# The second layer's linear-attention branch, moved tile by tile into the edge pass that sums gathered rows

## The reference

```python
def _L1_gnn_ref(x, edge_index, W, b):
    src = concat([edge_index[0], loop]); dst = concat([edge_index[1], loop])
    norm = deg_inv_sqrt[src] * deg_inv_sqrt[dst]
    h = x @ W.T
    out = segment_sum(h[src] * norm[:, None], dst, N) + b
    return relu(out)

def _L1_mix_ref(x, Wq, Wk, Wv, Wm, W1, W2, g1, b1, g2, b2):   # 8 heads of 32
    Q, K = elu(x @ Wq) + 1, elu(x @ Wk) + 1;  v = x @ Wv
    KV = einsum('nshd,nshv->nhdv', K, v)
    Z = 1 / (einsum('nlhd,nhd->nlh', Q, K.sum(axis=1)) + 1e-6)
    msg = layernorm(heads_joined(Q, KV, Z) @ Wm, g1, b1)
    msg = layernorm(relu(concat([x, msg]) @ W1) @ W2, g2, b2)
    return x + msg

xn = layernorm(x)
x = x + _L1_gnn_ref(xn, ...) + _L1_mix_ref(xn[None], ...)[0]
```

## Time and profile before

| what | value |
|---|---|
| median of three runs | 14292.15 us (14256.97 to 14311.86) |
| profiled execution | 14272.68 us, its span 14270.9 us |
| PE busy | 7573.7 us, 53% of the span |
| DVE busy | 6386.1 us, 45% |
| POOL busy | 6037.2 us, 42% |
| ACT busy | 1225.8 us, 9% |
| mean granted clock of PE | 0.773 of full speed |

### The profile page before, as it was taken

How to read it: one execution, slowest core, us unless ns; L and a number is a source line. 1 busy time by engine, 2 the same in 40 slices (tenths; PEclk the granted TensorE clock), 3 DMA queues, 4 the chain that set the end, 5 groups by cost and what they waited for, 6 DMA issues and landing times. The chain is left out here.

```text
span 14270.9 us, 106989 instructions
## 1 busy us (share of the span) xinstructions
PE 7573.7 (53%) x30362; PEld 6003.4 (42%) x30362; DVE 6386.1 (45%) x16883; ACT 1225.8 (9%) x3131; POOL 6037.2 (42%) x6226
## 2 busy tenths in 40 slices
PE   3334432556665455685555564555571955666534
PEld 3333332345554355553343432433351844555423
DVE  6555654467885322320000434666632134444454
ACT  0000000000001100110000111000010210110001
POOL 1666465056662266306666003666501016666000
PEclk9999999767777555697777787777785977777767
DMA  1111111055664011103336001112503313336100
GB/s 40 55 50 56 36 55 40 19 166 170 173 176 84 10 8 8 11 23 93 92 92 85 10 6 31 45 45 46 39 9 81 111 62 95 94 94 89 26 8 15
DMA packets 455094, 872.31 MB, mean 61 GB/s; under 512 B 171930, under 2 KB 267396, under 8 KB 454154
## 3 DMA queue, kind: packets, MB, share of 16 engines
q0 software_dynamic: 277568, 621.62, 20.3%
q1 hardware_dynamic: 176960, 244.01, 5.6%
HBM read 821.23 MB, written 52.88 MB: 61 GB/s over the span
## 5 line engine op out<-in xcount | busy, mean ns | idle before, releaser
L552 POOL DMA_INDIRECT ee_rows<-e_table,net_mr_data x1000 | 993.5, 993 | 1271.9 <-POOLq L1405 691.3
L817 POOL DMA_INDIRECT ce_rows<-c_table,net_mr_data x1000 | 948.2, 948 | 979.8 <-SPq L810 505.8
L552 POOL DMA_INDIRECT ge_rows<-g_table,net_mr_data x1000 | 961.0, 961 | 670.8 <-issue 233.1
L387 POOL DMA_INDIRECT main_slots<-em_load,em_where x784 | 808.9, 1032 | 641.9 <-DVE em_where L362 388.5
L552 POOL DMA_INDIRECT ae_rows<-a_table,net_mr_data x752 | 726.2, 966 | 590.7 <-POOLq L1405 200.7
L552 POOL DMA_INDIRECT be_rows<-b_table,b_br_data x728 | 703.1, 966 | 428.7 <-issue 176.8
L589 PE MATMUL ee_part_ps<-ee_message,net_eye 125*125 125x256 f32 x2000 | 588.8, 459 | 451.2 <-issue 258.3
L589 PE MATMUL ge_part_ps<-ge_rows,net_eye 125*125 125x256 f32 x2000 | 626.8, 482 | 308.2 <-issue 163.3
L346 PE MATMUL em_look_ps<-em_table,em_hot_tT 25*128 25x125 f32 x1568 | 366.9, 421 | 732.1 <-issue 662.6
L828 PE MATMUL ce_part_ps<-ce_rows,net_eye 125*125 125x256 f32 x2000 | 599.2, 452 | 289.9 <-issue 195.7
L589 PEld LDWEIGHTS ee_part_ps<-ee_message,net_eye 125*125 125x125 f32 x2000 | 461.1, 235 | 560.2 <-issue 467.6
(11 more groups left out here) (1010 smaller groups left out, 16655.6 us busy)
## 6 DMA issues: line engine op xcount, KB each, us to landing
em_key_row<-main_keys SPq DMA_DIRECT2D x98, 512.0 KB
f_w<-in_L_ffn_W_dram SPq DMA_DIRECT2D x40, 1024.0 KB
eg_key_row<-gat_keys SPq DMA_DIRECT2D x64, 512.0 KB
ce_rows<-c_table,net_mr_data POOLq DMA_INDIRECT x1000
ee_rows<-e_table,net_mr_data POOLq DMA_INDIRECT x1000
ge_rows<-g_table,net_mr_data POOLq DMA_INDIRECT x1000
main_slots<-em_load,em_where POOLq DMA_INDIRECT x784
ae_rows<-a_table,net_mr_data POOLq DMA_INDIRECT x752
```

Of the source, the lines that this page charges most:

```text
L387: pool.indirect_dma_start(edge["slots"], bass.IndirectOffsetOnAxis(ap=where[:, c:c + 1], axis=0), load[:, c, :], None).then_inc(scattered, 16)
L552: pool.indirect_dma_start(rows[n][:, s, :], None, table, bass.IndirectOffsetOnAxis(ap=data[:, g, s, 0:1].bitcast(I32), axis=0)).then_inc(g ...
L817: pool.indirect_dma_start(rows[:, g % RING, s, :], None, table, bass.IndirectOffsetOnAxis(ap=data[:, g, s, 0:1].bitcast(I32), axis=0)).the ...
```

## The change

The attention branch is no longer a row of stages behind the pass. `sum_pass` gets the rest of its work beside the 8 gathers of each group. A helper, `beside`, decides in turn i of every engine's loop which pieces run:

- from turn 2 on, one tile a turn: k and v of tile t in one product of 512 columns, its elu, and its share of the gram matrix (25 tiles, turns 2 to 28);
- in turn 29 the gram matrix is masked by heads on DVE (a mask made beforehand on POOL);
- from turn 29 on, one tile every 3 turns, cut into stages s0 to s11, each of which is one turn later than the one before it: q (s0), elu (s1), turn (s2), heads (s3), turn (s4), Wm and its statistics (s5), root and normalising (s5, s6), turn with gain and shift (s7), hidden layer (s8), output and statistics (s9), normalising (s10), the addition to `X` (s11). The last piece runs in turn 29 + 72 + 11 = 112 of 125.

All nine weight transfers are issued by SP at the start of the pass; ACT and DVE wait for all of them before their first group. `X` receives `A` and the last shift `b2` before the pass, in the same block in which the table is stored; the separate fill block is gone, and `close` keeps three of its four operations. On PE the pieces come behind `sum_slots(i)` and `total(i - 1)` in the turn, later stages before earlier ones; a piece waits for what ACT or DVE did with the same tile in the turn before. On DVE the addition to `acc` now comes one turn later in the loop.

```diff
--- before.py
+++ after.py
@@ -795,18 +795,56 @@
...
-def sum_pass(nc, edge, table, width, acc, const, name):
+def sum_pass(nc, edge, table, acc, XT, X, heads, weights, const, name):
...
-        rows = k.sb("rows", [128, RING, SLOTS, width])
-        hot, part = k.sb("hot", [128, HOTS, 2 * NP]), k.sb("part", [128, PARTS, width])
...
+        def beside(i, **stages):
+
+            if "gram" in stages and 0 <= i - FIRST - 2 < T:
+                stages["gram"](i - FIRST - 2)
+            if "keys" in stages and 0 <= i - FIRST - 1 < T:
+                stages["keys"](i - FIRST - 1)
+            if "kv" in stages and 0 <= i - FIRST < T:
+                stages["kv"](i - FIRST)
+            if "keep_gram" in stages and i == FIRST + T + 2:
+                stages["keep_gram"]()
+            for s in range(STAGES - 1, -1, -1):
+                t, off = divmod(i - SECOND - s, EACH)
+                if off == 0 and 0 <= t < T and f"s{s}" in stages:
+                    stages[f"s{s}"](t)
+
...
+            @block.sync
+            def _(sp):
+                for q, (to, of) in enumerate(((wkv[:, :, 0:D], "Wk"), (wkv[:, :, D:512], "Wv"), (wq[:, :, :], "Wq"), (wm[:, :, :], "Wm"))):
+                    sp.dma_start(to, weights[of].rearrange("(q p) n -> p q n", p=128)).then_inc(loaded, 16)
+                sp.dma_start(w1[:, :, :], weights["W1"][0, :, :].rearrange("(q p) n -> p q n", p=128)).then_inc(loaded, 16)
+                sp.dma_start(w2[:, :, :], weights["W2"][0, :, :].rearrange("(q p) n -> p q n", p=128)).then_inc(loaded, 16)
+                for to, of in ((g1, "g1"), (b1, "b1")):
+                    sp.dma_start(to[:, :], weights[of]).then_inc(loaded, 16)
+                sp.dma_start(g2[0:NP, :], along(weights["g2"], NP)).then_inc(loaded, 16)
+
+            LOADS = 16 * 9
+
...
+                def kv(t):
+                    if t == 0:
+                        pe.wait_ge(loaded, LOADS)
+                    if t >= 2:
+                        pe.wait_ge(k_made, t - 1)
+                    for q in range(2):
+                        ins = pe.matmul(bank[t % 2][0:NP, :], XT[:, q, tile(t)], wkv[:, q, :], start=(q == 0), stop=(q == 1))
+                    ins.then_inc(kv_made, 1)
...
+                def gram(t):
+                    pe.wait_ge(k_made, t + 1)
+                    pe.wait_ge(kv_out, t + 1)
+                    for m in range(2):
+                        ins = pe.matmul(bank[2 + m][:, 0:D + 1], k_t[0:NP, t % 2, m * 128:(m + 1) * 128], v_t[0:NP, t % 2, :], start=(t == 0), stop=(t == T - 1))
+                    ins.then_inc(grammed, 1)
...
+                def queries(t):
+                    if t == 0:
+                        pe.wait_ge(k_made, T)
+                    else:
+                        pe.wait_ge(qT_kept, t)
+                    times(bank[0][0:NP, 0:D], [XT[:, q, tile(t)] for q in range(2)], wq, q_made)
...
+                    pe.wait_ge(qT_kept, t + 1)
+                    if t == 0:
+                        pe.wait_ge(gram_kept, 1)
+                    else:
+                        pe.wait_ge(mT_kept, t)
+                    times(bank[1][0:NP, 0:D + 8], [qT[:, q, 0:NP] for q in range(2)], grams, m_made)
...
+                def mixed(t):
+                    pe.wait_ge(mT_kept, t + 1)
+                    if t:
+                        pe.wait_ge(nT_kept, t)
+                    times(bank[2][0:NP, 0:D], [mT[:, q, 0:NP] for q in range(2)], wm, w_made)
...
+                def hidden(t):
+                    pe.wait_ge(nT_kept, t + 1)
+                    if t:
+                        pe.wait_ge(y_kept, t)
+                    of = [XT[:, q, tile(t)] for q in range(2)] + [nT[:, q, 0:NP] for q in range(2)]
+                    for m in range(4):
+                        for q in range(4):
+                            ins = pe.matmul(bank[3][:, m * NP:(m + 1) * NP], w1[:, q, m * 128:(m + 1) * 128], of[q], start=(q == 0), stop=(q == 3))
+                    ins.then_inc(h_made, 1)
+
+                def outputs(t):
+                    pe.wait_ge(h_kept, t + 1)
+                    for q in range(4):
+                        ins = pe.matmul(bank[3][0:NP, 0:D], h_t[:, q, :], w2[:, q, :], start=(q == 0), stop=(q == 3))
+                    ins.then_inc(y_made, 1)
...
+                for i in range(G + 1):
+                    if i < G:
+                        sum_slots(i)
+                    if i:
+                        total(i - 1)
+                    beside(i, gram=gram, kv=kv, s0=queries, s2=turn_q, s3=heads_of, s4=turn_m, s5=mixed, s7=turn_n, s8=hidden, s9=outputs)
...
-                for g in range(G):
+                def keep_part(g):
                     act.wait_ge(slot_summed, (g + 1) * SLOTS)
...
+                def kv(t):
+                    act.wait_ge(k_low, t + 1)
+                    act.copy(v_t[0:NP, t % 2, 0:D], bank[t % 2][0:NP, D:512])
+                    act.activation(e_k[0:NP, t % 2, :], e_k[0:NP, t % 2, :], ACT.Exp).then_inc(kv_out, 1)
+
+                def exp_q(t):
+                    act.wait_ge(q_low, t + 1)
+                    act.activation(e_q[0:NP, :], e_q[0:NP, :], ACT.Exp).then_inc(q_exp, 1)
...
+                def root(t):
+                    act.wait_ge(asked, t + 1)
+                    act.activation(rstd[0][0:NP, :], rstd[0][0:NP, :], ACT.Sqrt).then_inc(given, 1)
...
+                def root2(t):
+                    act.wait_ge(asked2, t + 1)
+                    act.activation(rstd[1][0:NP, :], rstd[1][0:NP, :], ACT.Sqrt).then_inc(given2, 1)
...
+                act.wait_ge(loaded, LOADS)
+                for i in range(G):
+                    keep_part(i)
+                    beside(i, kv=kv, s0=exp_q, s2=keep_qT, s4=keep_mT, s5=root, s6=apply, s7=keep_nT, s8=keep_h, s9=root2, s10=apply2)
...
-                for g in range(min(4, G)):
-                    one_hot(g)
-                for g in range(G):
-                    if g + 4 < G:
-                        one_hot(g + 4)
...
+                def measure_y(t):
+                    dve.wait_ge(y_made, t + 1)
+                    measure(1, bank[3], asked2)
...
+                def keep_y(t):
+                    dve.wait_ge(y_kept, t + 1)
+                    dve.tensor_tensor(y_t[0:NP, :], y_t[0:NP, :], g2[0:NP, :], ALU.mult)
+                    dve.drain()
+                    dve.tensor_tensor(X[0:NP, t, :], X[0:NP, t, :], y_t[0:NP, :], ALU.add)
+                    dve.drain()
...
+                dve.memset(v_t[:, :, D:D + 1], 1.0)
+                dve.wait_ge(loaded, LOADS)
+                for g in range(min(4, G)):
+                    one_hot(g)
+                for i in range(G):
+                    if i + 4 < G:
+                        one_hot(i + 4)
+                    if i:
+                        add(i - 1)
+                    beside(i, kv=kv, keys=keys, keep_gram=keep_gram, s0=low_q, s1=keep_q, s3=keep_m, s5=measure_w, s6=finish_w, s9=measure_y, s10=finish_y, s11=keep_y)
+                add(G - 1)
 
...
 def layer1_graph(nc, I, X, inv_deg, edge, const):
     with Scope(nc, "c") as k:
-        XT = k.sb("XT", [128, 2, N])
+        XT, acc = k.sb("XT", [128, 2, N]), k.sb("acc", [128, T + 1, D])
...
-            A, acc = j.sb("A", [128, T, D]), j.sb("acc", [128, T + 1, D])
-            acc_all, acc = acc, acc[:, 0:T, :]
...
+            A, b2 = j.sb("A", [128, T, D]), j.sb("b2", [128, D])
...
-            on_vector(nc, "c_store", lambda dve: None, stores=[(table_rows(table[0:N, :]), acc[0:NP, :, :]), (table[N:N + 1, :], const["zeros"][0:1, 0:D])])
-            fill(nc, [(acc_all[:, T, :], 0.0)])
-            sum_pass(nc, edge, table, D, acc_all, const, "ce")
...
-                dve.tensor_tensor(X[0:NP, :, :], X[0:NP, :, :], A[0:NP, :, :], ALU.add)
-            on_vector(nc, "c_close", close, [(b_row[0:NP, :], along(I["L1_gnn_b"], NP))])
-        B, QT = k.sb("B", [128, T, D]), k.sb("QT", [128, 2, N])
...
-                project(nc, halves(XT), I["L1_mix_Wq"], D, put_rows(B), "c_q")
-                elu_plus_one(nc, B, E, NP, "c_eq")
-                turn_rows(nc, B, QT, const, "c_tq")
-                project(nc, halves(XT), I["L1_mix_Wk"], D, put_rows(B), "c_k")
-                elu_plus_one(nc, B, E, NP, "c_ek")
-                project(nc, halves(XT), I["L1_mix_Wv"], D, put_rows(V), "c_v")
-                fill(nc, [(V[:, :, D:D + 1], 1.0)])
...
-            gram(nc, B, V, G, "c_g", n_cols=D + 1)
...
-            keep_blocks(nc, [(0, G[:, 0, :], D), (128, G[:, 1, :], D)], 32, "c_b")
-            keep_head_columns(nc, G, 32, 8, D, "c_hc")
...
-            project(nc, halves(QT), None, 264, put, "c_m", weights_sb=G)
-        turn_rows(nc, B, QT, const, "c_tm")
-        project(nc, halves(QT), I["L1_mix_Wm"], D, put_rows(B), "c_wm")
-        tile_norm(nc, B, B, "c_n1", gain=I["L1_mix_g1"], shift=I["L1_mix_b1"])
-        turn_rows(nc, B, QT, const, "c_tn")
-        fill(nc, [(B[:, :, :], 0.0)])
```

(19 more changed lines are left out.)

173 lines of the change are left out of this document (137 added, 36 removed).

## The result

The changed kernel takes 13845.49 us (median of 4 runs, 13834.87 to 13890.8) against 14300.51 for the kernel before on the same chip: a ratio of 0.9694 over the runs, 95% interval 0.9668 to 0.9719 (the two medians alone give 0.968). The profiled execution took 13846.6 us, 426.1 less than that of before. Which of the two was the better reasoned is the question of the rest.

What follows compares the result with a forecast made beforehand. The pass was taken to go at POOL's gather pace, with single-file stages behind it. Terms -450 - 1 + 0 + 54 = -397 us gave 13895 us from 14292; the 8-in-10 range was 13815 to 14050 us.

Steps and rivals of the forecast that it cites:

- What goes: Behind the pass: the fourth operation of `close` and all thirteen stages vanish, the block's end gap stays; 450 us removed.
- Ahead of the pass: Before the gathers: two DVE operations and masks hide beside the table's store, the fill block goes (1.2 us); together -1 us.
- Weights: Start of the pass: nine transfers, 2.8 MB, beside the first gathers cost 0, upper end 20 us.
- PE, DVE, ACT beside the gathers: Inside the pass: PE averages 7.3 of 11.4 us a turn; neither DVE nor ACT reaches a third of 1461 us.
- What the pass grows by: The gather pass lengthens by 54 us, scaled from pass `ge` by PE's added work; ends 0 and 152 us.
- The picture behind it: In the pass, some 170 us of POOL's waiting come from occasionally late PE signals, mostly covered by four buffers.
- The port rule: In the pass, two-input DVE additions in SBUF could block GpSimd's making of gathers; at its strongest some 20 us more.
- Rival 1: The pass doesn't notice the added work, POOL stays at 1.42 us a step: 13841 us; chance 0.17.
- Rival 2: In-order exchange: late PE signals hold up three engines in the pass, 13993 us up to some 14060; chance 0.22.
- Rival 3: PE becomes the pass's bound at a low clock and the kernel gets slower, 14417 us; chance 0.04.
- Rival 4: The work stretches every turn of the pass by its own time, PE's 294 us in full: 14135 us; chance 0.06.

Runs made afterwards that it cites:

- no_pieces: Changed kernel with every piece of the branch left out of the pass, weight transfers kept: 13809.35 us, ratio 0.9673 to the kernel before.
- before_ring5: Kernel before with five gather buffers in place of four: 14299.89 us, ratio 1.0011 to the kernel before.
- free_gathers: Changed kernel whose gathers wait for no sum, PE's sums reading a weight block instead of gathered slots: 14438.64 us, ratio 1.0106 to the kernel before.
- phase1_only: Changed kernel with only the branch's first phase (keys, values, gram matrix), turns 29 on left out: 13825.72 us, ratio 0.9687 to the kernel before.
- one_slot: Changed kernel where PE adds only the last of each group's eight slots and signals once: 13842.64 us, ratio 0.9697 to the kernel before.
- dve_two: Changed kernel with one more two-input DVE addition in SBUF per turn, results unused: 13876.79 us, ratio 0.9731 to the kernel before.

## Why the prediction was right, and where it wasn't

- **What goes, 450 us**: right; the stages are gone and the gap at the block's end even shrank by 1.0 us.
- **Ahead of the pass, -1 us**: +1.0 measured. The two DVE operations (6.76 and 6.83 us) and the masks lie beside the store, as said. The fill's 1.2 us did not appear as a gain.
- **Weights, 0**: right, by no_pieces and by where POOL first stops: its first pause stands at the seventh group, 61 us after the first gather, in the timeline of the changed kernel. The kernel before has its first pause at the same gather, 3.3 us long.

```profile
6447.40 0.94 POOL L855 DMA_INDIRECT ce_rows<-c_table,net_mr_data  x1 [0.30 <-issue]
6452.37 0.94 POOL L855 DMA_INDIRECT ce_rows<-c_table,net_mr_data  x1 [4.03 <-remote]
```

- **PE, DVE, ACT beside the gathers**: PE's busy time 1029 us (forecast about 1040), clock 0.80 (over 0.72); DVE's 247 lies under the 306 that I allowed; 47 table loads in the second phase and one before it, 1283 ns each, free.
- **What the pass grows by, 54 us**: the mis-sized term. The gathers grew by 20.5, all of it from the second phase. The further 6.6 us at the end aren't the pieces': no_pieces, without any piece, has 46.9 us there, before_ring5, an edit of the kernel before, 47.0, and the kernels with one shared zero row lie between 39.4 and 47.0, free_gathers apart. With 20 for 54 the sum gives 13861, and what is left to 13845 is inside the scatter between executions. So that the forecast of 13895 came within 50 us rests on the 450 us that go. Scaling from `ge` by PE's work was the failing step: phase1_only adds 60 us of PE's busy time and nothing to the pass, one_slot takes some 320 us from PE and gives nothing back.
- **The picture behind it**, that PE is now and then late and that four buffers cover most of it, is refuted by before_ring5, and free_gathers put another in its place: gathers hold back PE or its signals. The forecast took the lateness for smaller than it was. The copy that starts at 6562.87 belongs to the sum begun at 6549.62, 9.6 us after its records end; the sum begun at 6553.94 is copied at 6586.81, 29 us after its own. The forecast's reason that work on PE lengthens the pass survives only as what was measured, 20 us for the second phase.
- **Rival 1** (the pass doesn't notice) has the better number for the median, 13841, but the gathers did notice: its 1421 us came out for the first phase alone. Rivals 2, 3 and 4 would have needed gathers over 1560 us; the clock rose instead of falling. Rival 3's danger is real in another form: where POOL doesn't pause, PE takes 5.6 us a product at a clock of 0.51, and the kernel does become 1.1% slower than before.
- **The port rule** I priced at up to 20 us inside the pass. The changed kernel's own gathers show 1.6 us; the rule's case of two inputs is borne out by dve_two and by the masks (below).

Open: why the second phase costs 20 us and the first none; why the pauses are as long with an eighth of PE's sums; whether the gathers hold PE's work or its signals; and what makes one chip free of all this.

## What to carry to other kernels

Work in single file behind a pass that is bound by gathers is worth moving beside it even on the engine that seems to hold the gathers: 450 us of stages cost 20 there. Before a wait is called lateness, lengthen the ring once: if nothing moves, the releaser may be held back by the very engine that waits. Then take the wait away once, as free_gathers does, before the pauses are cut: here they were to be kept. And look at the stretch at a list's end by itself; slots that all point at one row cost this kernel with its five passes some 93 us.
